# Flamingo block on one core: four blocks of 512 tokens with the FFN inside the head slots, instead of two halves with the FFN at their end

## What is computed

```python
x = x + tanh(g_xattn) * attention(layernorm(x), ctx) @ Wo
#   q = layernorm(x) @ Wq, k = ctx @ Wk, v = ctx @ Wv   (512 -> 32 heads x 128)
#   probs = softmax(q k^T / sqrt(128) + pair_bias, masked), 64 x 64 per batch and head
x = x + tanh(g_ffn) * (layernorm(x) @ Wf^T + bias + lora(layernorm(x)))
#   lora: one of 3 adapters of rank 16, chosen per batch, none for some batches
```

## Time and profile before

| | |
|---|---|
| time, median of 3 runs | 1893.93 us (1893.77 to 1894.58) |
| span of the profiled execution | 1893.1 us (the profile gives no other time of it) |
| instructions | 30362 |
| PE, PEld busy | 1826.3, 1615.6 us |
| DVE, ACT, POOL busy | 1174.6, 659.6, 790.2 us |
| DMA | 99.6 MB, mean 53 GB/s |

### The profile page before, as it was taken

One profiled execution on the slowest core, in us unless ns is written; L12 is line 12 of the kernel. 1 busy time (PEld: TensorE's weight loads), 2 busy tenths in 40 slices (PEclk: granted clock), 3 DMA queues, 4 the chain that ended last, 5 costly groups with the idle time before them and its releaser, 6 DMA issues.

```text
span 1893.1 us, 30362 instructions
## 1 busy us (share of the span) xinstructions
PE 1826.3 (96%) x10656; PEld 1615.6 (85%) x10656; DVE 1174.6 (62%) x2178; ACT 659.6 (35%) x1216; POOL 790.2 (42%) x872
## 2 busy tenths in 40 slices
PE   4899999999999999999879999999999999999988
PEld 4788888888888888888669888888888888888876
DVE  4866666666666666666756666666666666666674
ACT  3333333333333333333223333333333333333331
POOL 2343434444444444444324434344444444444423
PEclk9999999999999999999889999999999999999999
DMA  4211111111111111101231011111111011111001
GB/s 156 79 56 50 44 55 55 50 36 41 55 50 54 46 55 50 48 30 56 67 111 69 29 50 55 50 44 55 55 50 42 36 55 50 55 44 55 17 1 45
DMA packets 37343, 99.60 MB, mean 53 GB/s; under 512 B 5136, under 2 KB 5392, under 8 KB 37312
## 3 DMA queue, kind: packets, MB, share of 16 engines
q1 hardware_dynamic: 35136, 96.09, 15.1%
q10 hardware_dynamic: 2176, 3.10, 0.5%
HBM read 94.98 MB, written 4.19 MB: 52 GB/s over the span
## 4 chain that ended last, share of the span: by engine, by line
PE 94%; DVE 4%; ACT 1%; issue 1%; ACTq 1%; POOL 0%; DVEq 0%; POOLq 0%
PE vo_bank L174 13%; PE vo_bank L176 13%; PE vo_bank L175 13%; PE q_bank L174 7%; PE q_bank L175 7%; PE q_bank L176 7%; PE k_bank L174 6%; PE k_bank L176 6%; PE k_bank L175 6%; PE s_two L196 3%; PE s_two L197 3%; PE pv_two L196 3%; PE pv_two L197 3%; PE pv_two L323 3%; ACTq L533 1%
## 5 line engine op out<-in xcount | busy, mean ns | idle before, releaser
L886 POOL TENSOR_TENSOR shifted<-score,row_max 128x256 f32<-128x256 f32 x128 | 78.5, 613 | 795.7 <-DVE row_max L650 795.7
L174 PE MATMUL vo_bank<-wv_hi,ct_hi 128*128 128x256 f32 x1024 | 295.4, 289 | 18.9 <-POOL wv_lo L841 18.9
L176 PE MATMUL vo_bank<-wv_hi,ct_lo 128*128 128x256 f32 x1024 | 290.7, 284 | 0.0
L175 PE MATMUL vo_bank<-wv_lo,ct_hi 128*128 128x256 f32 x1024 | 290.5, 284 | 0.0
L629 DVE TENSOR_TENSOR acc<-vo_bank,acc 128x512 f32<-128x512 f32 x256 | 176.9, 692 | 93.6 <-PE vo_bank L176 90.4
L174 PEld LDWEIGHTS vo_bank<-wv_hi,ct_hi 128*128 128x128 f32 x1024 | 197.0, 192 | 21.3 <-issue 18.9
L841 POOL TENSOR_TENSOR ot_lo<-attn,ot_hi 128x512 fp32r<-128x512 f32 x128 | 165.3, 1291 | 118.4 <-ACT ot_hi L438 118.4
L174 PE MATMUL vo_bank<-wo_hi,ot_hi 128*128 128x512 f32 x512 | 207.2, 405 | 7.2 <-DVE acc L629 5.5
L174 PE MATMUL q_bank<-xt_hi,wq_hi 128*128 128x512 f32 x512 | 203.0, 396 | 2.8 <-DVE xt_lo L600 2.8
L175 PE MATMUL q_bank<-xt_lo,wq_hi 128*128 128x512 f32 x512 | 202.0, 394 | 0.0
L176 PE MATMUL vo_bank<-wo_hi,ot_lo 128*128 128x512 f32 x512 | 201.6, 394 | 0.0
(11 more groups left out here) (128 smaller groups left out, 4011.3 us busy)
## 6 DMA issues: line engine op xcount, KB each, us to landing
raw_q<-in_wq SPq DMA_DIRECT2D x31, 512.0 KB, 3.3
raw_k<-in_wk SPq DMA_DIRECT2D x31, 512.0 KB, 4.9
raw_v<-in_wv SPq DMA_DIRECT2D x31, 512.0 KB, 5.7
raw_bias<-in_pair_bias SPq DMA_DIRECT2D x62, 256.0 KB, 2.6
raw_o<-in_wo SPq DMA_DIRECT2D x31, 512.0 KB, 3.2
stage<-in_ctxt SPq DMA_DIRECT2D x16, 256.0 KB, 4.4
acc<-in_x SPq DMA_DIRECT2D x16, 256.0 KB, 4.2
out<-y_out SPq DMA_DIRECT2D x16, 256.0 KB, 2.0
```

What stands on the lines that cost most here:

```text
L174: pe.matmul(to, left[0], right[0], start=first, stop=False)
L175: pe.matmul(to, left[0], right[1], start=False, stop=False)
L176: return pe.matmul(to, left[1], right[0], start=False, stop=last)
L886: pool.tensor_tensor(shifted[:, :, :], score[:, :, :], row_max[:, :].unsqueeze(2).to_broadcast([P, PB, S]), ALU.subtract).then_inc(shift_d ...
```

## The change

The kernel is written anew around the same products.

- Four blocks of 512 tokens are gone through one after the other, 32 heads each, 128 slots in all (`SLOTS`), one head a slot. There are two `xt`, two `ct` and two `acc`, by the parity of the block. No hardware loop is left, all slots are written out.
- Head groups are of four (G = 4). A group's values are made a tile at a time for four heads (12 matmuls of 512 columns a tile), two tiles in slot 3 of the group before and two in slot 0; its outputs, four heads deep, are made two tiles in slot 1 and two in slot 2 of the next group. Every slot so has two jobs of 12 matmuls of 512 columns. `v` has three half buffers, `ot` five buffers.
- `wq` and `wk` are loaded and rounded for one head a slot, in single buffers; `wv` and `wo` in pieces of 256 KB through two buffers `raw_vo`, two pieces a slot. Each weight is now read four times.
- `prob` is 128 x 256 without zeros, and ScalarE's exp writes into it; two transposes turn it, and ScalarE and VectorE copy the two diagonal blocks into `pt`, in two instructions each. `shifted`, `bias_m`, `score_b`, `expd` are made in place. The batches of a pair are now m and m + 4 of a block, so copies of `q_bank` and `k_bank` rearrange.
- The FFN of block b-1 (sums in slots 3 and 4, turns of `xn` in 5 to 8, inner LoRA product in 9 and 10, dense in 11 to 14, with the store) and the first norm of block b+1 (sums in 17 and 18, turns and context pieces in 19 to 22) lie inside the slots of block b, on the same two `vo_bank`s. The gates are applied in `row_scale` and `rstd` rather than in the weights, the bias is a row of `b_w`, and the result is added in `acc` and stored from there.
- Block 0's first norm stands ahead of slot 0, block 3's FFN behind slot 127.

```diff
@@ sizes and schedule
-HALVES = 2
-T = NB * S // HALVES
-HG = 2
-G = H // HG
-STAGES = BLOCKS * HG
+BLOCKS = NB * S // BLK
+G = 4
+GROUPS = BLOCKS * H // G
+SLOTS = BLOCKS * H
+OT_BUFS = 5
+def turn_at(n):
+    b, s = divmod(n, H)
+    if n < SLOTS and b > 0 and 5 <= s < 9:
+        return FFN, b - 1, s - 5
+    if n < SLOTS and b < BLOCKS - 1 and 19 <= s < 23:
+        return LEAD, b + 1, s - 19
...
+def values_at(n):
+    if n % G == G - 1 and n < LAST:
+        return n // G + 1, (0, 1)
+    if n % G == 0 and 0 < n < SLOTS:
+        return n // G, (2, 3)
...
+def output_at(n):
+    if n % G in (1, 2) and n > G and n < SLOTS:
+        return n // G - 1, (0, 1) if n % G == 1 else (2, 3)
@@ SyncE
+            def head(m):
+                wait(sp, wq_lo, m)
+                load(flat(raw_q[:, :, :]), wq[m % H], raw_q_in)
+                wait(sp, wk_lo, m)
+                load(flat(raw_k[:, :, :]), wk[m % H], raw_k_in)
+            def raw_pair(n):
+                i, g = n % G, n // G
+                for k in range(2):
+                    if i in (1, 2) and g + 1 < GROUPS:
+                        piece = 2 * (i - 1) + k
+                        wait(sp, wo_lo, G * (g - 1) + 2 + k + 1 if i == 1 else 0)
+                        wait(sp, wv_lo, G * (g + 1) + k + 1 if i == 2 else 0)
+                        load(raw_vo[k][:, :], wv[C * ((g + 1) % (H // G)) + piece], raw_vo_in[k])
...
+            for n in range(SLOTS):
+                b, s = divmod(n, H)
+                if n + 2 < SLOTS:
+                    head(n + 2)
+                if n % 2 == 0 and 2 <= n < SLOTS - 2:
+                    bias(n // 2 + 1)
+                if n > 0:
+                    raw_pair(n + 1)
+                at = piece_at(n)
+                if at:
+                    piece(at[0] + 2)
+                if dense_at(n):
+                    store(*dense_at(n))
@@ TensorE
+            def values(g, t):
...
+                wait(pe, vo_free, NUMBER[job] - 1)
+                for c in range(C):
+                    mm = mm3(pe, bank_of(job)[:, :], parts(ct[b % 2], slice(None), c, cols(t, P)),
+                             parts(v_w, slice(None), c, slice(None)), c == 0, c == C - 1)
+                mm.then_inc(vo_ps, 1)
...
             def probabilities(n):
-                for p in range(PB):
-                    mm = pe.transpose(t_bank[:, cols(p, P)], prob[:, p, :], ident[:, :])
+                for j in range(2):
+                    mm = pe.transpose(t_bank[:, cols(j, P)], flat(prob[:, cols(j, 2), :]), ident[:, :])
...
+            def slot(n):
+                if n > 0:
+                    queries(n)
+                    keys(n)
+                    main_job(n, 0)
+                    probabilities(n - 1)
+                    main_job(n, 1)
+                if turn_at(n):
+                    turn(*turn_at(n))
+                if lora_at(n):
+                    lora_inner(*lora_at(n))
+                if dense_at(n):
+                    dense(*dense_at(n))
+                scores(n)
+                if n > 0:
+                    attention(n - 1)
@@ ScalarE
+            def weights_vo(n):
+                i, g = n % G, n // G
+                for k in range(2):
+                    if i in (1, 2) and g + 1 < GROUPS:
+                        act.wait_ge(raw_vo_in[k], 16 * raw_count(n))
+                        act.wait_ge(vo_ps, NUMBER["v", g, PB - 1] + 1)
+                        hi(v_w[0][:, 2 * (i - 1) + k, :], raw_vo[k][:, :], wv_hi)
...
+            def slot(n):
+                if n > 0:
+                    queries(n)
+                if n < LAST:
+                    weights_q(n + 1)
+                if n > 0:
+                    keys(n)
+                if n < LAST:
+                    weights_k(n + 1)
+                weights_vo(n)
+                if n > 0:
+                    main_job(n, 0)
+                    probabilities(n - 1)
+                    main_job(n, 1)
...
+                if n > 0:
+                    attention(n - 1)
                 exps(n)
@@ VectorE
+            def slot(n):
+                if n > 0:
+                    queries(n)
+                    keys(n)
+                weights_o(n)
+                if sums_at(n):
+                    statistics(*sums_at(n))
+                if turn_at(n):
+                    normalise(*turn_at(n))
+                if n > 0:
+                    main_job(n, 0)
+                    probabilities(n - 1)
+                    main_job(n, 1)
+                if turn_at(n):
+                    turn(*turn_at(n))
...
+                scores(n)
+                if n > 0:
+                    attention(n - 1)
+                if lora_at(n):
+                    lora_rest(*lora_at(n))
+                row_scales(n)
@@ GpSimd
-                for b in range(2):
-                    rows = cols(b, S)
-                    last = pool.tensor_tensor(prob[rows, :, rows], expd[rows, :, :],
-                                              row_scale[rows, :].unsqueeze(2).to_broadcast([S, PB, S]), ALU.mult)
-                last.then_inc(prob_done, 1)
+                pool.tensor_tensor(prob[:, :, :], prob[:, :, :],
+                                   row_scale[:, :].unsqueeze(2).to_broadcast([P, PB, S]), ALU.mult).then_inc(prob_done, 1)
+            def slot(n):
+                if n % H == 0:
+                    masks(n // H)
+                add_bias(n)
+                if n < LAST:
+                    weights_q(n + 1)
+                    weights_k(n + 1)
+                weights_v(n)
+                if sums_at(n):
+                    deviations(*sums_at(n))
+                shift(n)
+                if n > 0:
+                    attention(n - 1)
+                probabilities(n)
```

More of the change, by code:

```diff
@@ new lines, in _ @@
+            pe.wait_ge(ident_done, 2)
+            for t in range(PB):
+                values(0, t)
+            keys(0)
+            for t in range(PB):
+                turn(LEAD, 0, t)
+            queries(0)
+            for n in range(SLOTS):
+                slot(n)
+            probabilities(LAST)
+            attention(LAST)
+            for t in range(PB):
+                output(GROUPS - 1, t)
+            for t in range(PB):
+                turn(FFN, BLOCKS - 1, t)
+            for p in range(2):
+                lora_inner(BLOCKS - 1, p)
@@ new lines, in _ @@
+            act.wait_ge(g1_in, 16)
+            act.activation(gate[:, :], g_in[:, :], ACT.Tanh).then_inc(gate_done, 1)
+            for t in range(PB):
+                values(0, t)
+            keys(0)
+            for t in range(PB):
+                turn(LEAD, 0, t)
+            queries(0)
+            for n in range(SLOTS):
+                slot(n)
+            probabilities(LAST)
+            weights_vo(SLOTS)
+            attention(LAST)
+            for t in range(PB):
+                turn(FFN, BLOCKS - 1, t)
@@ L597, in _ @@
+            for p in range(2):
+                lora(BLOCKS - 1, p)
         @block.vector
@@ new lines, in _ @@
+            for pair in range(2):
+                statistics(LEAD, 0, pair)
+            normalise(LEAD, 0, 0)
+            normalise(LEAD, 0, 1)
+            for t in range(PB):
+                values(0, t)
+            keys(0)
+            for t in range(PB):
+                turn(LEAD, 0, t)
+                if t < 2:
+                    normalise(LEAD, 0, t + 2)
+            queries(0)
+            dve.wait_ge(mask_in, 16)
+            dve.tensor_reduce(row_kept[:, :], mask_u8[:, :, :], X, ALU.max).then_inc(kept_done, 1)
@@ new lines, in _ @@
+            dve.wait_ge(kept_done, 1)
+            constants()
+            for n in range(SLOTS):
+                slot(n)
+            probabilities(LAST)
+            weights_o(SLOTS)
+            attention(LAST)
+            for pair in range(2):
+                output(GROUPS - 1, 2 * pair)
+                output(GROUPS - 1, 2 * pair + 1)
+                statistics(FFN, BLOCKS - 1, pair)
+            normalise(FFN, BLOCKS - 1, 0)
+            normalise(FFN, BLOCKS - 1, 1)
+            for t in range(PB):
+                turn(FFN, BLOCKS - 1, t)
+                if t < 2:
+                    normalise(FFN, BLOCKS - 1, t + 2)
@@ L838, in _ @@
+            for p in range(2):
+                lora_gate(BLOCKS - 1, p)
+                lora_rest(BLOCKS - 1, p)
+            for t in range(PB):
+                dense(BLOCKS - 1, t)
         @block.gpsimd
```

1187 lines of the change are left out of this document (544 added, 643 removed).

## The result

| | median us | lowest to highest | ratio to before, 95% interval |
|---|---|---|---|
| before | 1894.26 (4 runs) | 1893.77 to 1895.71 | |
| after | 1823.94 (4 runs) | 1822.91 to 1823.99 | 0.9627 [0.9613, 0.9641] |

The account below looks back on a forecast made before the run. PE, busy 96% of the span, was taken as the bound; start 69, 125 slots of 13.13 us (1641), norms and FFN 64 and end 57 gave 1831 us of span, 1832 us forecast; likeliest range 1820 to 1848, 8-in-10 range 1816 to 1862.

Parts of the forecast that it names:

- The step that was mis-sized: transposes: Probability transposes in each slot: going from four to two saves 0.18 us, at most 0.22.
- Value matmuls: Values in the slots: 369 us become 350, 19 us less; a fixed 2.5 ns a matmul would save only 4.
- Loop: Hardware loop around the slots of the kernel before: it costs nothing one can see.
- What must stay hidden: Added rounding and loads on other engines in each slot: hidden behind PE, costed at nothing; softmax chain leaves 2.9 us.
- Norms and FFN inside slots: Three FFNs and three first norms inside slots: 62 us of PE work plus 2 us for delays, 64 us.
- Start: Before the steady slots: PE begins at about 14 us, slot 3 at about 69, 8 us either way.
- End: Behind slot 127: softmax, outputs, statistics, turns, LoRA, dense and store sum to 56.6 us.
- The cross-check: Whole span: 173 us outside slots become 150; 40 us gained from slots, 22 between the halves and at the ends.
- Some slots stall: Slots with turns, sums or `raw_vo` exchange: 0.2 to 0.4 us on each slot, 1857 to 1880 us; chance 0.10.
- Slower through `raw_vo`: Exchange of the two `raw_vo` buffers exceeds 8.6 us and lengthens every slot; 2007 us at 10 us; chance 0.06.
- No change: Whole kernel: the gain falls to the same stalls, 1890 to 1898 us; chance 0.03.
- More than forecast: Turns, LoRA and cold starts overlap better, start reached earlier: 1810 to 1820 us; chance 0.08.

Follow-up runs that it names:

- the first experiment: Changed kernel with its values made in two halves of 256 columns instead of matmuls of 512 columns; 1839.08 us, ratio 0.9711 to the kernel before.
- its two mended forms: Changed kernel with sums behind attention, context loaded first and adapter constants spread, 1819.74 us; the same plus last outputs made head by head, 1811.34 us.
- the kernel above: Changed kernel with each low part of the value weights computed three times by GpSimd, twice into scratch; 1851.42 us, ratio 0.9774 to the kernel before.

## Why the prediction came out as it did

**Right in mechanism, the gain 8 us too small (62 forecast, 70 measured).** The likeliest case held, near the lower end of its own range of 1820 to 1848. The sum was 69 + 1641 + 64 + 57 = 1831 us of span. Measured in the same order it is 69.5 + 125 x 13.073 (1634.1) + 64.6 + 54.0 = 1822.2. Two terms carry the difference: 7 us from the slot and 3 from the end.

- *The step that was mis-sized: transposes.* "Two save 0.18 us, at most 0.22" was the step. I halved the 0.35 us of four. They save 0.23: an O slot was 13.307 before and is 13.073. The time of four is not twice that of two (0.35 and 0.13), and an error of 0.05 us counts 125 times. The late matmul behind them, of which I was to decide whether it goes too, stays (0.09 in both).
- *Value matmuls.* Predicted 3072 x 0.120 against 1536 x 0.228, 0.15 us for each slot on average; a V slot against an O slot showed 0.26 to 0.27 before, and the first experiment 0.28 for two jobs, 0.14 a slot on average. Right; the fixed part of 2.5 ns a matmul, which would have given 1847, does not hold for this stream.
- *Loop.* Costed at nothing, measured 0.9999 [0.999, 1.0009]. The changed kernel reads 72 + 57 instruction packets and 1.65 MB, and its slots are alike to 0.01 us to the end (slot 126 is 13.07).
- *What must stay hidden.* It stays hidden in all regular slots, though VectorE was busier than said. The softmax chain ends at +5.3 as worked out: the probabilities of slot 12 start at 204.88 and the slot after begins at 200.19, so they end at 205.5. No wait of PE or ScalarE on `raw_vo` is in the table of waits. The longest waits of PE after are:

```profile
PE vo_bank L272 <- POOL wv_lo L929: 15.3, 1, 15.3
PE pv_two L437 <- POOL prob L983: 7.7, 2, 4.5
...
PE pv_two L277 <- DVE pt L734: 5.1, 7, 1.9
```

- *Norms and FFN inside slots.* "64", measured 64.6, with its parts in other places. Dense slots are 16.49 (3.42 more, predicted 3.43), the two LoRA slots together 2.95 more (2.9). A turn adds 0.44, not 0.54: 0.36 for its four transposes and 0.08 for the late matmul, where I had taken 0.44 for the four and 0.1 for the matmul. That four turns still come to the predicted 2.1 us is luck, since slots 20, 39 and 40 take 0.36, 0.15 and 0.22 us more than that. "PE's work is all that counts there" was wrong for the slots with sums, to which I gave nothing: slots 35 and 36 take 0.36 and 0.47 us too long (the sums in slots 49 and 50 cost nothing). The chain in slot 36:

```profile
510.75 2.16 DVE wo_lo L689 x2
512.91 1.21 DVE stats L774 x2
...
514.39 0.57 DVE v_lo L689
...
515.87 0.35 PE pv_two L277
```

  The prediction has no row for a `wo_lo`; with the 0.69 us of a `v_lo` the pair would take 1.38. It takes 2.16, the statistics stand behind it, `pt` is late and PE waits. Over the kernel the sum slots lose 2.5 us by this. The chain of slot 20 begins its delay in the same way, with a `wo_lo` of 1.78 us. A row of the kernel before could have told it; 1235 ns is its mean:

```profile
L603 DVE SCALAR_TENSOR_TENSOR wo_lo<-raw_o,gate,wo_hi 128x512 fp32r<-128x512 f32 x64 | 76.5, 1235 | 28.8 <-ACT wo_hi L438 28.8
```

- *Start.* "Slot 3 at about 69" held (69.46) because two errors cancel. PE starts at 15.27, not 14, since a context piece lands only at 12.67. VectorE's constants end earlier than I thought: it takes slot 0's scores from 47.68, not 50.6, and attention of head 0 ends with slot 1 at 57.60, not 60. But slot 2 takes 11.9 us where I had 9: its first six queries run at the low clock, 0.43 us each, which is 1.2 of the 2.9, and PE waits for the softmax chain behind it.
- *End.* Predicted 56.6 behind slot 127, measured 54.0. Slot 127 has no job, so that the last outputs start at 1778.16, 3.1 us sooner than my sum; the statistics take 2 us instead of 4. The LoRA product takes 4.8 us instead of 2.3, since after the wait for the last turns PE's clock is at its low level for 1800.24 to some 1804.5.

```profile
1778.16 0.80 PE vo_bank L272
...
1792.08 0.69 DVE acc L719
...
1800.24 0.58 PE vo_bank L272
```

**The cross-check** put 40 us on 128 slots and 22 on what lay outside; counted in the same way it is 46.9 and 24.1 (by the table, with 121 slots, 44.3 and 26.7). Of the 26.7, 9.1 are the border, and the experiment with the gathered FFN shows 8.0 us for the spreading alone. The 9.1 at the start and 8.5 at the end, either of them uncertain by about 1 us, I put down to a block of 512 tokens in place of a half of 1024, with fewer turns and dense tiles outside the slots; no run separates them.

**The rivals.** *Some slots stall*: true of some sum and turn slots, but for tenths in a few places and not on every slot. (0.4 us on each slot would have been 1882 us, not the 1880 of the prediction.) *Slower through `raw_vo`*: nothing waits for it; the slack is about 5 us of GpSimd in two of four slots, and with 7.7 us more in each of them the kernel is 5% slower than before, so that side was real but far, and reached by another wait. *No change*: out. *More than forecast* (1810 to 1820) was not reached by this kernel, but its two mended forms run at 1819.7 and 1811.3. It stays open what in the new order makes slot 51 longer. Nor was the exchange of `raw_vo` itself tried, with a third buffer or a slower load.

## What to carry to other kernels

Where PE is the bound and one slot repeats a hundred times, read the slot from the starts of its matmuls, price an edit by the difference of two such slots and not by a share of one duration, and look for fewer and wider matmuls: each one saved is worth 12 ns here, each transpose about 0.12 us. Work at the borders is worth spreading over steady slots, but by what its open round trips measure, 2.6 to 2.7 us a block here, and not by one for every step. Follow every queue with the durations that its instructions have in company, and read the groups of the operations that the change makes more frequent: in slots 20 and 36, whose chains were read, the delay began with an operation that was slower beside its neighbour than alone.

## What was not expected of the hardware

**A VectorE product with both operands in SBUF is slow beside GpSimd.** `wo_lo` and `v_lo` are the same shape; `v_lo` reads one operand from PSUM. Groups by shape on VectorE (busy us, mean ns, idle before):

```profile
L689 DVE TENSOR_TENSOR wo_lo<-raw_vo,wo_hi 128x512 fp32r<-128x512 f32 x128 | 143.7, 1161 | 21.6 <-ACT wo_hi L527 21.5
...
L689 DVE TENSOR_TENSOR v_lo<-vo_bank,v_hi 128x512 fp32r<-128x512 f32 x128 | 87.6, 684 | 57.7 <-ACT v_hi L527 57.2
```

1161 against 684 ns. The timelines of both engines in slot 12 of the changed kernel, then at 1762 us, where GpSimd has nothing to do:

```profile
194.52 2.25 DVE L689 TENSOR_TENSOR wo_lo<-raw_vo,wo_hi 128x512 fp32r<-128x512 f32 x2 [0.35 <-ACT wo_hi L527]
...
194.33 1.29 POOL L929 TENSOR_TENSOR wk_lo<-raw_k,wk_hi 128x512 fp32r<-128x512 f32 x1
...
1762.14 1.28 DVE L689 TENSOR_TENSOR wo_lo<-raw_vo,wo_hi 128x512 fp32r<-128x512 f32 x2
```

The pair takes 1.28 us alone and 2.25 beside `wk_lo`; it ends at 196.77, which is 1.15 us behind the end of `wk_lo` (195.62): as if the first of the two had stood still until GpSimd was done. The 128 single `wo_lo` of the changed kernel bear this out. 77 start while GpSimd makes a low part, and every one of them ends 0.54 to 0.55 us behind the end of GpSimd's operation, whatever its own start; they take 0.97 to 1.78 us. The other 51 take 0.68 to 0.69. `kt`, the same operation with one operand in PSUM, starts 97 times beside such a GpSimd operation and takes 0.69 us each time. One of these in slot 12, beside `wq_lo`:

```profile
193.47 0.69 DVE L689 TENSOR_TENSOR kt<-k_bank,kt 128x512 fp32r<-128x512 f32 x1 [1.15 <-ACT kt L527]
...
193.07 1.30 POOL L929 TENSOR_TENSOR wq_lo<-raw_q,wq_hi 128x512 fp32r<-128x512 f32 x1
```

With three products on GpSimd (the kernel above) a pair stands between two GpSimd operations, and both sides pay:

```profile
134.28 3.24 DVE L690 TENSOR_TENSOR wo_lo<-raw_vo,wo_hi 128x512 fp32r<-128x512 f32 x2 [0.34 <-ACT wo_hi L528]
...
133.98 1.29 POOL L930 TENSOR_TENSOR wq_lo<-raw_q,wq_hi 128x512 fp32r<-128x512 f32 x1
135.23 1.74 POOL L930 TENSOR_TENSOR wk_lo<-raw_k,wk_hi 128x512 fp32r<-128x512 f32 x1
```

The first `wo_lo` waits for `wq_lo` (to 135.27) and then holds `wk_lo` up, which takes 1.74 us instead of 1.29; the second waits for `wk_lo` (to 136.97) and ends 0.55 us later, at 137.52. The Trainium skill (SBUF — State Buffer, section "Who interferes with whom") says that a VectorE instruction with two SBUF inputs contends with a GpSimd instruction that reads SBUF, over shared ports that are an exclusive lock, and that the order of issue decides who blocks; these rows agree with it, with 1.0 us for the pair. All this is read from traces; no run here moved `wo_lo` away from GpSimd's products.

**Transposes are not proportional.** Four fp32 transposes of 128 x 128 took 0.35 us of PE, two 0.13 us, with a matmul of 512 columns behind them late by 0.09 us in both; two more in every slot cost 0.23 us a slot.
